# Transposing o_n at the head of the next step, with its copy behind qT, in a pipelined transformer block

## What is computed

```python
x = x + 0.5 * ffn_ref(layernorm(x), ...)
x = x + attn_ref(layernorm(x), ...)
x = x + 0.5 * ffn_ref(layernorm(x), ...)
```

```python
h = shift_token(x)                         # upper half of the channels from the token before
q, k, v = split(h @ wqkv, 3)               # 8 heads of 64
q, k = rotary_xpos(l2norm(q) * qs, l2norm(k) * ksc)
o = local_attention(q, k, v)               # windows of 64 tokens, own window and the one before
x = x + o.reshape(b, n, 512) @ wo
h = layernorm(shift_token(x)) * lg + lb
a, g = split(h @ w1 + b1, 2)
x = x + (a * gelu(g)) @ w2 + b2
```

## Time and profile before

| | |
|---|---|
| median of 3 runs | 1897.68 us (1894.85 to 1900.1) |
| profiled execution | 1896.57 us |
| its span, first to last instruction | 1894.4 us |
| PE busy | 1534.4 us, 81% |
| PEld busy | 1241.7 us, 66% |
| DVE busy | 1391.3 us, 73% |
| ACT busy | 1102.6 us, 58% |
| POOL busy | 1091.3 us, 58% |
| mean granted TensorE clock | 0.945 |

### The profile page before, as it was taken

The page is one execution under the profiler, slowest core; times in us unless marked ns, Lnnn a source line. Parts: engine busy times, 40 slices in busy tenths (PEclk is TensorE's granted clock), DMA queues, the critical chain, the costliest instruction groups (busy, mean ns, idle before and its releaser), DMA issues.

```text
span 1894.4 us, 44270 instructions
## 1 busy us (share of the span) xinstructions
PE 1534.4 (81%) x15864; PEld 1241.7 (66%) x15864; DVE 1391.3 (73%) x3642; ACT 1102.6 (58%) x2291; POOL 1091.3 (58%) x1090
## 2 busy tenths in 40 slices
PE   1889999978999999656747658899998889999984
PEld 1677777767777777535535446777776777777763
DVE  6687979776879797355665647979796778788773
ACT  1576767666767676312213216767676667677671
POOL 3686858565858585131221217858585658577660
PEclk9899999989999999878879779999999999999997
DMA  8142212222222121031010022212223222212113
GB/s 272 45 121 49 52 45 64 56 78 67 53 49 51 49 51 38 18 125 45 0 44 22 0 72 49 55 45 51 50 61 89 51 67 50 51 42 55 43 35 113
DMA packets 183659, 112.32 MB, mean 59 GB/s; under 512 B 86720, under 2 KB 164128, under 8 KB 182944
## 3 DMA queue, kind: packets, MB, share of 16 engines
q1 hardware_dynamic: 183456, 109.65, 22.1%
HBM read 43.41 MB, written 23.42 MB: 35 GB/s over the span
## 4 chain that ended last, share of the span: by engine, by line
PE 51%; DVE 26%; issue 7%; ACT 6%; SPq 3%; DMA 3%; POOL 2%; DVEq 0%; POOLq 0%; ACTq 0%
PE QK L332 9%; PE TO L568 9%; PE QK L568 5%; PE TO L635 5%; DVE rope_c L932 5%; DVE o_n L957 4%; DVE rope_s L937 4%; PE TO L332 3%; DVE top L878 3%; PE SC L609 3%; DVE h2n L944 3%; PE TO L681 2%; PE TO L735 2%; PE VB L735 2%; ACT probs L1080 2%
## 5 line engine op out<-in xcount | busy, mean ns | idle before, releaser
L1080 ACT ACTIVATE probs<-SC,shift,qgain 128x128 f32<-128x128 f32 x1024 | 389.6, 480 | 102.4 <-DVE shift L886 102.1
L1204 POOL TENSOR_TENSOR ve<-mv,epsilon 128x1 f32<-128x1 f32 x128 | 24.3, 190 | 400.3 <-DVE mv L923 400.3
L332 PE MATMUL QK<-w_qkv,hT 128*128 128x512 f32 x768 | 222.1, 426 | 20.9 <-DMA w_qkv<-qkv_d 11.4
L932 DVE TENSOR_TENSOR rope_c<-QK,rope 128x512 f32<-128x512 f32 x256 | 175.7, 686 | 78.5 <-PE QK L332 75.8
L1217 POOL TENSOR_TENSOR rnorm<-clip,mhalf 128x8 f32<-128x8 f32 x128 | 210.9, 1648 | 12.8 <-DVE clip L895 12.6
L1226 POOL TENSOR_TENSOR qgain<-clip,mhalf 128x8 f32<-128x8 f32 x128 | 209.2, 1635 | 0.0
L568 PE MATMUL TO<-ident,probs 128*128 128x128 f32 x1280 | 189.0, 275 | 17.9 <-ACT probs L1080 11.2
L878 DVE TENSOR_REDUCE top<-SC 128x4 f32<-128x512 f32 x256 | 174.7, 682 | 31.7 <-PE SC L609 31.4
L1231 POOL TENSOR_TENSOR q_r<-rope_c,rope_s 128x512 f32<-128x512 f32 x128 | 163.0, 1273 | 49.3 <-DVE rope_s L937 49.3
L937 DVE TENSOR_TENSOR rope_s<-QK,rope 128x256 f32<-128x256 f32 x512 | 191.0, 415 | 0.0
L568 PEld LDWEIGHTS TO<-ident,probs 128*128 128x128 f32 x1280 | 152.3, 141 | 57.4 <-issue 27.4
(11 more groups left out here) (135 smaller groups left out, 3818.7 us busy)
## 6 DMA issues: line engine op xcount, KB each, us to landing
v_prev<-v_own SPq DMA_DIRECT2D x256, 130.0 KB, 2.3
x_att<-stream SPq DMA_DIRECT2D x128, 64.0 KB, 2.3
h<-stream SPq DMA_DIRECT2D x256, 32.0 KB, 1.9
stream<-x_new SPq DMA_DIRECT2D x32, 256.0 KB
w_qkv<-qkv_d SPq DMA_DIRECT2D x3, 1536.0 KB, 7.9
h<-x_mid SPq DMA_DIRECT2D x128, 32.0 KB
h<-x_mid SPq DMA_DIRECT2D x128, 31.8 KB
rope<-rope_d SPq DMA_DIRECT2D x24, 128.0 KB, 3.1
```

What stands on the lines that cost most here:

```text
L332: last = mm(dst, fr(left(a)), fr(right(b)), start=(k == 0), stop=(k == 2))
L932: v.tensor_tensor(qk(rope_c[:])[:, m], src, rope[:, i, m, 0:1, :].to_broadcast([P, HEADS, DH]), ALU.mult)
L1080: last = nc.scalar.activation(probs[:, b, hd, :], SC[:, hd * P:hd * P + P], ACT.Exp, bias=shift[:, b, hd:hd + 1], scale=qgain[:, b, hd % 4 ...
```

## The change

The transposes of o_n for a tile are taken from the end of the step in which the tile is in ATT and put into the step that follows, in which it is in WO: behind the transposes of k_r and q_r, ahead of the first half of the probabilities. The wait for `s_xn` behind a burst goes with them, since they are now the first to write OB. ScalarE's copy of oT goes from the end of its step to the place behind qT in the next one, ahead of the second half of the exponentials. As the burst writes over TO, it now waits for `s_on` itself. The cut in the QKV block only splits one condition in two.

```diff
@@ TensorE, step @@
                             last.then_inc(s_tqk, 1)
+                    if t := tile(WO):
+                        pe.wait_ge(s_on, t.count())
+                        if before is not None:
+                            pe.wait_ge(s_xn, before * 2 + 2)
+                        for c in range(PAIRS):
+                            last = transpose(OB[:, c * P:c * P + P], o_n[:, c * P:c * P + P])
+                        last.then_inc(s_to, 1)
                     if t := tile(ATT):
                         probs_transposed(t, 0)
                     if t := tile(WO):
                         if t.i == 0:
                             pe.wait_ge(s_wow, t.loads() * 16)
                         pe.wait_ge(s_oT, t.count())
-                        if before is not None:
-                            pe.wait_ge(s_xn, before * 2 + 2)
                         for c in range(PAIRS):
...
                         transpose(VB[:, P:2 * P], h2n[:, t.i % 2, :]).then_inc(s_th2, 1)
-                    if t := tile(ATT):
-                        pe.wait_ge(s_on, t.count())
-                        for c in range(PAIRS):
-                            last = transpose(OB[:, c * P:c * P + P], o_n[:, c * P:c * P + P])
-                        last.then_inc(s_to, 1)
                     if burst is not None:
                         ffn(tile, burst)
...
             def ffn(tile, n):
                 last_in = tile(FFN_IN)
+                if t := tile(ATT):
+                    pe.wait_ge(s_on, t.count())
                 pe.wait_ge(s_ffnw, last_in.loads() * 96 - 15)
...
                     elif t := tile(ATT):
-                        pe.wait_ge(s_oT, t.count())
+                        pe.wait_ge(s_on, t.count())
@@ ScalarE, step @@
                     copy(qT[:, b], QK[:, 0:512].rearrange("d (c t) -> d c t", c=PAIRS)).then_inc(s_qT, 1)
+                if t := tile(WO):
+                    act.wait_ge(s_to, t.count())
+                    need(act, s_y, t.count(back=1))
+                    copy(oT[:], OB[:].rearrange("d (c t) -> d c t", c=PAIRS)).then_inc(s_oT, 1)
                 if t := tile(ATT):
                     exponentials(t, 1)
...
-                if t := tile(ATT):
-                    act.wait_ge(s_to, t.count())
-                    need(act, s_y, t.count(back=1))
-                    copy(oT[:], OB[:].rearrange("d (c t) -> d c t", c=PAIRS)).then_inc(s_oT, 1)
                 if burst is not None:
```

More of the change, by code:

```diff
@@ L652, in f @@
                                     lambda x: w_qkv[:, x, m * 512:m * 512 + 512]).then_inc(signal, 1)
+                    if t := tile(QKV):
+                        b = t.i % 2
                         if t2 := tile(FFN_IN + 1):
```

## The result

| | before | after |
|---|---|---|
| median of 4 runs beside each other | 1898.18 us (1894.85 to 1900.1) | 1985.74 us (1982.2 to 1988.25) |
| ratio after / before, 95% interval | | 1.0462 (1.044 to 1.0484) |
| profiled execution | 1896.57 us | 1988.25 us |
| its span | 1894.4 us | 1986.1 us |
| mean granted TensorE clock | 0.945 | 0.945 |

The account below looks back on a forecast made before the run. The bound was the loop of exponentials, ScalarE's copies, output projection, q and k products, rotation, h2n and maximum. 47.1 + 20.2 + 9.0 + 7.1 + 1.2 = 84.6 us on 1896.57 gave 1981 us, range 1946 to 1996.

Parts of the forecast that it names:

- TensorE's hole is worth nothing: TensorE idles 0.82 us a step waiting for o_n; filling that with the k and q transposes was to gain nothing.
- The copy goes from the first place to the third: ScalarE was to copy kT, qT, oT in that order, making the output projection 0.76 us late in each step.
- Steps of 9.95 us: The step of 9.19 us was to grow by 0.76 us, the delay of the output projection.
- first pattern: 62 tiles with 9.19 us steps, products queued behind the projection and h2n taking 1.19 us; 0.76 us each, 47.1 us.
- The second pattern falls into the first: 24 tiles with 9.11 us steps and h2n of 0.34 us were to take 9.95 us: 0.84 each, 20.2 us.
- Bursts: 14 feed-forward bursts: projection 1.11 us late behind x_new, less 0.47 for a saved ScalarE place: 0.64 each, 9.0 us.
- the 12 steps behind them: Steps following a feed-forward burst, 9.36 us long, were to become 9.95: 0.59 us each, 7.1 us together.
- h2n comes free: Rival: GpSimd's k_r moves later, so VectorE's h2n no longer waits; 0.31 us a step, 35 us, total 1946; chance 0.10.
- Two tiles wait for w_o and hide the delay: Two tiles whose projection waits for w_o, 4.9 us together, were priced at nothing, with a bound of 0.76 each.
- The other tiles that were held hidden: Two tiles waiting for w_qkv, two for k_a, and four at the stacks' ends: priced at nothing.
- The first tile of each stack: The two stacks' first tiles were priced like steps behind a burst: 0.59 us each, 1.2 us together.

Follow-up runs that it names:

- e1: The changed kernel with ScalarE's copy oT moved first, ahead of kT and qT, TensorE's new order kept: 1910.29 us, ratio 1.007 to the kernel before.
- e3: The kernel before with only ScalarE's copy oT moved behind qT in the next step, except in burst steps; TensorE's order old: 2005.17 us, ratio 1.0557.
- e4: The changed kernel with GpSimd's qgain put ahead of k_r, so k_r begins later: 1961.75 us, ratio 1.0333 to the kernel before.
- f4: The changed kernel with a second buffer for w_o, the second layer's weights loaded a sequence ahead: 1979.01 us, ratio 1.042 to the kernel before.
- e2: The changed kernel with ScalarE's copy oT between kT and qT: 1933.86 us, ratio 1.0192 to the kernel before.
- f1: e1 with burst steps as in the kernel before, o_n transposes and copy oT at their end: 1890.9 us, ratio 0.9952 to the kernel before.
- f2: f1 with VectorE's low part of hT moved ahead of the norms' reduction: 1877.84 us, ratio 0.9889 to the kernel before.
- f3: The kernel before with only VectorE's low part of hT moved ahead of the norms' reduction: 1890.57 us, ratio 0.9958.

## Why the prediction was right

The forecast, 1981 us, is 4.7 under the median of after, and the mechanism is the one forecast. Point by point:

- *TensorE's hole is worth nothing.* Held: the transposes of o_n end while ScalarE is still busy with other work. e1 puts a number to it, 0.08 us a step.
- *The copy goes from the first place to the third, and the projection starts 0.05 us behind it.* Held: oT starts 0.95 us later against the exponentials than in the earlier trace rows, two places of 0.475, and the hand-over is 0.05. e1 to e3 show that the step follows the place; e4 shows that 0.29 us of the 9.96 is h2n's wait, which the kernel before has too.
- *Steps of 9.95 us.* 9.96. The 63 tiles of the first pattern lose 0.79 each on average, 49.5 us in all (forecast 47.1).
- *The second pattern falls into the first.* Held: 23 tiles lose 0.80 each on average, 18.4 us (20.2). The prediction had counted 62 and 24 for these 63 and 23. h2n was short in 42 tiles before and is in 14 after; its mean is 1.09 us.
- *Bursts.* The 14 lose 0.57 each on average, 8.0 us (9.0); the 12 steps behind them 0.63, 7.6 us (7.1). In the changed kernel's trace behind a burst x_new ends at 378.55 and the projection starts 1.46 us later, between the 1.42 and 1.53 of the prediction:

```profile
377.86 0.69 DVE L910 TENSOR_TENSOR x_new<-TO,x_b 128x512 f32<-128x512 f32 x1 [1.99 <-PE TO L738]
378.70 0.63 PE L568 MATMUL TO<-ident,o_n 128*128 128x128 f32 x4
379.36 0.60 ACT L1077 ACTIVATE oT<-TO 128x512 f32<-128x512 f32 x1
380.01 1.16 PE L640 MATMUL TO<-w_o,oT 128*128 128x128 f32 x8 [0.25 <-ACT oT L1077]
```

- *h2n comes free* did not come about: in the step above it starts 0.07 us ahead of k_r, as in the earlier trace rows, since both follow the projection. e4 shows that the price of that rival was right. One of the prediction's reasons against it, that the one that starts first holds the ports, doesn't hold here: h2n starts first and still waits (last section).
- *Two tiles wait for w_o and hide the delay* is the term that failed. They were priced at nothing, with 0.76 as the bound, and lost 2.88 each on average, 5.8 us (steps 12.11 and 11.83 became 14.95 and 14.75). The bound took it that the wait's end would stay and the work behind it keep its length. The end stayed (5.45 us behind the exponentials, from 5.50 in the first of them); the work behind it got longer, while the granted clock was 0.50 (last section). f4 shows the term by itself: with w_o there in time both steps are plain ones.
- The other tiles that were held hidden: those that wait for w_qkv gained 0.79 each, those that wait for k_a are unchanged, the stacks' four end tiles gained 0.1 each. The first tile of each stack lost 1.66 us where 0.59 was put down; the cause is open.

The classes sum up to 90.4 us: 49.5 + 18.4 + 8.0 + 7.6 + 3.3 (first tiles) + 5.8 (w_o) - 1.6 (w_qkv) - 0.5 (ends), to within rounding. The start, the attention between the stacks and the end add 1.3, and 91.7 is the difference of the spans. Of the 7.1 us that the forecast lacks, w_o is 5.8; the other misses, up to 2.4 us each, come to 1.3 together, since they lie on both sides. That they nearly cancel is luck.

## What to carry to other kernels

Idle time ahead of an instruction is a price only if its reader could start earlier: walk from the wait to the next engine, and count what a copy's place in an in-order queue is worth there (here 0.475 us a place, three places, three step lengths). The two halves of one change can have different signs; here TensorE's half gains 0.08 us a step with the copy kept first, and the copy's half loses the rest, so try each half alone. A stretch that is priced at nothing because a wait hides the delay can still get longer: the work behind the wait need not keep its length.

## What was not expected of the hardware

**The clock and an idle stretch.** In the step that waits for w_o, the changed kernel's TensorE (timeline, then the engines' busy time in stretches) shows this:

```profile
459.51 2.07 PE L640 MATMUL TO<-w_o,oT 128*128 128x128 f32 x8 [3.24 <-DMA w_o<-wo_in]
...
461.23 2.91 PE L332 MATMUL QK<-w_qkv,hT 128*128 128x512 f32 x6
```

```profile
core 0: us, PE busy (x) PEld busy (x) DVE busy (x) ACT busy (x) POOL busy (x), PEclk, DMA share, GB/s
452.00:458.90 6.90, 4.24 (x74) 3.29 (x66) 5.62 (x14) 5.87 (x15) 5.10 (x4) 1.00 0.44 105
458.90:465.70 6.80, 6.19 (x20) 5.22 (x21) 3.08 (x9) 0.24 (x1) 3.46 (x5) 0.50 0.01 2
```

The granted clock falls from 1.00 to 0.50, from 2.4 to 1.2 GHz, at 458.9, 0.6 us ahead of the wait's end, and stays there for 6.8 us: the projection takes 2.07 us where the plain step has 1.16 and the products 2.91 where it has 1.65. In the kernel before, the same place has two idle pieces, and the clock stays:

```profile
430.02 0.66 PE L568 MATMUL TO<-ident,o_n 128*128 128x128 f32 x4 [0.74 <-DVE o_n L957]
...
434.48 1.16 PE L635 MATMUL TO<-w_o,oT 128*128 128x128 f32 x8 [2.49 <-DMA w_o<-wo_in]
...
434.40:441.00 6.60, 6.52 (x89) 5.24 (x89) 4.87 (x12) 2.44 (x3) 4.71 (x6) 1.00 0.19 44
```

TensorE idles 0.74 + 2.49 = 3.23 us there, 3.24 in one piece after, since the transposes of o_n no longer stand between. What the fall costs, e4 shows in one kernel, whose two w_o steps have the same idle time ahead of the projection (a row of the timeline, then a stretch, in which the granted clock is the third number from the end):

```profile
447.12 1.16 PE L640 MATMUL TO<-w_o,oT 128*128 128x128 f32 x8 [2.70 <-DMA w_o<-wo_in]
447.50:450.90 3.40, 3.40 (x23) 2.79 (x21) 2.15 (x6) 0.47 (x1) 2.04 (x4) 1.00 0.00 0
...
1555.01 1.74 PE L640 MATMUL TO<-w_o,oT 128*128 128x128 f32 x8 [2.69 <-DMA w_o<-wo_in]
1555.40:1558.80 3.40, 3.40 (x13) 2.92 (x13) 1.01 (x4) 0.00 (x0) 1.48 (x4) 0.50 0.02 5
```

The first step takes 11.88 us, the second, with 3.4 us at 0.50, takes 13.43. In the profiled executions the clock falls in 11 of the 12 w_o steps with the new order on TensorE (the changed kernel, e1, e2, e4, f1, f2) and in 1 of the 6 with the old one (before, e3, f3). So the new order goes with the fall, but that one longer idle piece causes it is not shown: f3, with pieces of 0.74 and 2.46 us as in before, has one step in which the clock falls (14.13 us), and e4 one in which it stays. The cause of the fall stays open.

**Which GpSimd instruction holds VectorE up.** In the step of e4 above, h2n runs in its short 0.34 us while GpSimd's 1.64-us qgain on 128x8 is under way; beside the 128x512 k_r it lasts 1.20 us in the changed kernel. The Trainium skill, SBUF — State Buffer, section SBUF: two separate sides, has the one that starts first hold the shared ports for the whole instruction while the other blocks. By that h2n, which starts 0.04 us behind qgain, would have waited for its end, 1.6 us; it didn't, and the measurement decides: beside k_r h2n is held up, beside qgain it is not. The order of the recorded starts differs from that rule too: in the first pattern h2n starts 0.07 us ahead of k_r and still ends 0.08 us behind it.
